# A fused linear, sigmoid and linear layer on one core: W2 staged through y, new places for Pool's loads, b2 added a stage sooner

## The reference

```python
# x: (1024, 24, 1024), W1: (1024, 24), b1: (1024,), W2: (1024, 1024), b2: (1024,), all float32
h = jax.nn.sigmoid(jnp.einsum('bts,st->bs', x, W1) + b1)
return h @ W2.T + b2
```

## Time and profile before

| | us |
|---|---|
| median of 3 runs | 336.53 |
| lowest, highest | 336.32, 337.71 |
| the profiled execution | 337.88 |
| its span, first to last instruction | 336.1 |

### The profile page before, as it was taken

The page is one execution under the profiler, slowest core; times in us unless marked ns, Lnnn a source line. Parts: engine busy times, 40 slices in busy tenths (PEclk is TensorE's granted clock), DMA queues, the critical chain, the costliest instruction groups (busy, mean ns, idle before and its releaser), DMA issues.

```text
span 336.1 us, 4849 instructions
## 1 busy us (share of the span) xinstructions
PE 273.2 (81%) x1825; PEld 238.0 (71%) x1825; DVE 259.1 (77%) x386; ACT 44.5 (13%) x76; POOL 165.5 (49%) x63
## 2 busy tenths in 40 slices
PE   2672975696977989999993899998889979299896
PEld 2572965596966877889782788876778868188674
DVE  0652997987998979799993489899788997168836
ACT  1210220211260000012300000040101140000010
POOL 0050007679059684800899980049755059972000
PEclk9978797977999999999997699999999998789979
DMA  8999959999999999999957999999999992698006
GB/s 260 398 398 393 387 183 393 386 387 387 386 386 387 387 387 387 387 384 373 373 205 244 374 375 384 383 385 374 373 373 372 356 341 81 207 345 262 1 0 250
DMA packets 67383, 109.99 MB, mean 327 GB/s; under 512 B 3224, under 2 KB 40096, under 8 KB 67360
## 3 DMA queue, kind: packets, MB, share of 16 engines
q1 hardware_dynamic: 65584, 106.96, 89.3%
q10 hardware_dynamic: 1776, 2.72, 2.2%
HBM read 105.48 MB, written 4.19 MB: 326 GB/s over the span
## 4 chain that ended last, share of the span: by engine, by line
PE 36%; DMA 35%; POOL 14%; issue 10%; ACT 2%; SPq 1%; DVE 1%; POOLq 0%; DVEq 0%; ACTq 0%
DMA ring<-in_r_x 35%; PE xbank L207 17%; PE pbank L267 15%; POOL y L463 6%; POOL nsum L446 3%; PE xbank L301 3%; POOL h_lo L456 2%; POOL nsum L451 1%; POOL nat L448 1%; PE pbank L301 1%; ACT h L392 1%; SPq L171 1%; DVE acc L323 1%; ACT h_hi L421 0%; PE pbank L225 0%
## 5 line engine op out<-in xcount | busy, mean ns | idle before, releaser
L323 DVE SCALAR_TENSOR_TENSOR acc<-xbank,w,acc 128x512 f32<-128x512 f32 x304 | 213.6, 746 | 57.1 <-PE xbank L207 54.5
L207 PE MATMUL xbank<-ident,ring 128*128 128x128 f32 x1280 | 190.8, 286 | 54.5 <-DMA ring<-in_r_x 53.6
L207 PEld LDWEIGHTS xbank<-ident,ring 128*128 128x128 f32 x1280 | 162.2, 149 | 83.2 <-issue 33.0
L448 POOL TENSOR_TENSOR nat<-nat,w1all 128x2048 f32<-128x2048 f32 (+2 forms) x15 | 55.1, 3674 | 50.7 <-DMA nat<-in_r_x 50.7
L451 POOL TENSOR_TENSOR nsum<-nsum,nat 128x2048 f32<-128x2048 f32 (+2 forms) x15 | 55.4, 3692 | 1.2
L267 PE MATMUL pbank<-w_hi,h_hi 128*128 128x512 f32 x112 | 51.7, 462 | 0.0
L267 PE MATMUL pbank<-w_lo,h_hi 128*128 128x512 f32 x112 | 50.8, 454 | 0.0
L456 POOL TENSOR_TENSOR h_lo<-h,h_hi 128x512 fp32r<-128x512 f32 x14 | 17.5, 1283 | 67.5 <-ACT h_hi L421 67.5
L267 PE MATMUL pbank<-w_hi,h_lo 128*128 128x512 f32 x112 | 45.6, 454 | 0.0
L446 POOL TENSOR_TENSOR nsum<-nat,w1all 128x2048 f32<-128x2048 f32 (+2 forms) x5 | 18.5, 3699 | 18.7 <-DMA nat<-in_r_x 18.7
L392 ACT ACTIVATE h<-acc,b1col 128x512 f32<-128x512 f32 (+1 forms) x19 | 11.0, 646 | 104.1 <-DVE y L339 57.7
(11 more groups left out here) (38 smaller groups left out, 94.7 us busy)
## 6 DMA issues: line engine op xcount, KB each, us to landing
ring<-in_r_x SPq DMA_DIRECT2D x40, 1024.0 KB, 14.4
ring<-in_r_x SPq DMA_DIRECT2D x40, 768.0 KB, 11.6
ring<-in_r_x SPq DMA_DIRECT2D x20, 512.0 KB, 7.5
nat<-in_r_x SPq DMA_DIRECT2D x8, 1024.0 KB, 14.2
nat<-in_r_x SPq DMA_DIRECT2D x8, 768.0 KB, 10.0
y<-in_L_rec_W SPq DMA_DIRECT2D x1, 2048.0 KB, 18.3
out_y<-y ACTq DMA_DIRECT2D x4, 512.0 KB, 6.8
nat<-in_r_x SPq DMA_DIRECT2D x4, 512.0 KB, 6.6
```

Of the source, the lines that this page charges most:

```text
L207: mm = pe.transpose(xbank[u % XBANKS][:, j * P:(j + 1) * P], tile[:, j, :], ident[:, :])
L323: nc.vector.scalar_tensor_tensor(out=acc[:, c, :], in0=xbank[u % XBANKS][:, :], scalar=w1[:, bass.ds((STAGES[i][1] + c) * T + t, 1)], in1= ...
L448: nc.gpsimd.tensor_tensor(slot, slot, row, ALU.mult).then_inc(nat_weighed, 1)
```

## The change

- STAGES gets the number of row tiles of a stage and a word for the fate of its outputs ("keep" in y, "add" to y, "last": add and store). Rows and chunks of the five stages stay as they were, and so do the fates.
- The places of Pool's four loads become (2, 4, 10, 14) in stage 0 and (0, 3, 10, 14) in the others. They were (3, 11, 15, 19) and (1, 6, 11, 16).
- W1 is the first load on SP's queue; it was the first on ACT's.
- W2's first half is loaded into y after place 1 and its second half into y after place 17 of stage 0, once SP has seen the eighth transpose of the first. Nothing of W2 goes through h and nat any more, and the wait of load m = 1 is gone. The transposes of W2 stand at units 14, 17, ..., 35 and 58, 61, ..., 79 (they stood at 12, 15, ..., 57); the second set of w1all rows stands between the two halves, at units 38 to 44 (it stood at 65 to 71).
- steps_due: the window begins at the same unit (10), but has 4/5 len - 10 units in place of len - 13: 57, 40, 40 and 23 units for 71, 50, 50 and 29.
- add_b2 stands ahead of low_parts in stages 1 and 3, and waits for the two kept outputs of a row tile and not for all eight.
- In the tail both chunks of the last h are made in pieces of 128 rows; it was the first chunk alone.

```diff
 STAGES = (
-    (0, 0, 4, (3, 11, 15, 19)),
-    (0, 4, 4, (1, 6, 11, 16)),
-    (1, 0, 3, (1, 6, 11, 16)),
-    (1, 3, 3, (1, 6, 11, 16)),
-    (1, 6, 2, (1, 6, 11, 16)),
+    (0, 4, 0, 4, (2, 4, 10, 14), "keep"),
+    (0, 4, 4, 4, (0, 3, 10, 14), "last"),
+    (4, 4, 0, 3, (0, 3, 10, 14), "keep"),
+    (4, 4, 3, 3, (0, 3, 10, 14), "add"),
+    (4, 4, 6, 2, (0, 3, 10, 14), "last"),
 )
...
         def steps_due(i, v):
 
-            lead, rest = 10, 3
-            span = len(units[i]) - lead - rest
-            return max(0, min(product_steps(i), -(-(v - lead + 1) * product_steps(i) // span)))
+            steps = outs[i - 1] * 3 * chunks[i - 1]
+            lead = 10 * JT // tiles[i]
+            span = (len(units[i]) * 4) // 5 - lead
+            return max(0, min(steps, -(-(v - lead + 1) * steps // span)))
...
-        W2_FROM, W2_EVERY = 12, 3
         SETS = {4 + q: q for q in range(1 + NK)}
-        SETS.update({65 + 2 * q: 1 + NK + q for q in range(NK)})
+        SETS.update({38 + 2 * q: 1 + NK + q for q in range(NK)})
+        W2S = {14 + 3 * m if m < SC else 58 + 3 * (m - SC): m for m in range(OH * SC)}
 
         @block.sync
         def _(sp):
+            sp.dma_start(w1[:, :].rearrange("p (c t) -> p c t", t=T),
+                         W1.rearrange("(c p) t -> p c t", p=P)).then_inc(w1_loaded, 16)
...
                     if at in places:
-                        if m == 1:
-                            sp.wait_ge(w2_turned, SC)
                         if m >= NATS:
                             sp.wait_ge(nat_freed, m - NATS + 1)
...
                     if i == 0 and at == 1:
-                        sp.dma_start(h[:, :, :].rearrange("p (j a) b -> p j (a b)", j=2), w2_v[1][:, 0:2, :]).then_inc(w2_loaded[1], 16)
-                        sp.dma_start(nat[:, 1, :, :].rearrange("p (j a) b -> p j (a b)", j=2), w2_v[1][:, 2:4, :]).then_inc(w2_loaded[2], 16)
-                    if i == 0 and at == 4:
                         sp.dma_start(y[:, :, :], w2_v[0]).then_inc(w2_loaded[0], 16)
+                    if i == 0 and at == 17:
+                        sp.wait_ge(w2_turned, SC)
+                        sp.dma_start(y[:, :, :], w2_v[1]).then_inc(w2_loaded[1], 16)
...
-            def add_b2(g):
+            def add_b2(b):
                 pool.wait_ge(b2_loaded, 16)
-                pool.wait_ge(part_kept, (g + 1) * OUTS)
                 for j in range(JT):
+                    pool.wait_ge(part_kept, kept_at[b] + OH * (j + 1))
                     nc.gpsimd.tensor_tensor(y[:, j, :], y[:, j, :], b2all[:, :], ALU.add).then_inc(b2_added, 1)
 
             for i in range(NS):
                 weighted_sum(i)
+                if i > 0 and fate[i - 1] == "keep":
+                    add_b2(i - 1)
                 if i < LAST:
                     low_parts(i)
-                if i in (1, 3):
-                    add_b2(i // 2)
```

More of the change, by code:

```diff
@@ L39, in rec_kernel @@
     XBANKS = 6
-    assert (B, T, S, O) == (2 * BANK, 24, 1024, 1024) and OUTS == 8
-    chunks = [s[2] for s in STAGES]
+    assert (B, T, S, O) == (2 * BANK, 24, 1024, 1024)
+    tiles = [s[1] for s in STAGES]
+    chunks = [s[3] for s in STAGES]
+    wide = [n * P for n in tiles]
+    fate = [s[5] for s in STAGES]
     units = []
-    ts = list(range(NK, T))
-    for g, c0, n, places in STAGES:
-        order = [("x", t, c) for t in ts[:-2] for c in range(n)]
+    for n in chunks:
+        order = [("x", t, c) for t in range(NK, T - 2) for c in range(n)]
         order += [("n", 0, c) for c in range(n)]
-        order += [("x", t, c) for t in ts[-2:] for c in range(n)]
+        order += [("x", t, c) for t in range(T - 2, T) for c in range(n)]
         units.append(order)
@@ L54, in rec_kernel @@
     first_h = [sum(chunks[:i]) for i in range(NS)]
+    outs = [OH * n for n in tiles]
+    first_out = [sum(outs[:i]) for i in range(NS)]
+    kept_at = [sum(n for n, f in zip(outs[:i], fate) if f == "keep") for i in range(NS)]
+    added_at = [sum(n for n, f in zip(outs[:i], fate) if f != "keep") for i in range(NS)]
     item_of, item_end = {}, []
     for i in range(NS):
-        for t in ts:
+        for t in range(NK, T):
             item_of[i, t] = len(item_end)
@@ L64, in chunk_end @@
         return first_unit[i] + max(v for v, (_, _, cc) in enumerate(units[i]) if cc == c) + 1
-    x_v = x.rearrange("(g j p) t s -> g p j t s", p=P, j=JT)
-    out_v = out.rearrange("(g j p) o -> g p j o", p=P, j=JT)
+    x_v = x.rearrange("(j p) t s -> p j t s", p=P)
+    out_v = out.rearrange("(j p) o -> p j o", p=P)
     w2_v = W2.rearrange("(h j p) s -> h p j s", p=P, j=JT)
@@ L97, in rec_kernel @@
         nat_loaded = [sem(f"nat_loaded{n}") for n in range(NATS)]
-        w2_loaded = [sem(f"w2_loaded{n}") for n in range(3)]
+        w2_loaded = [sem(f"w2_loaded{n}") for n in range(OH)]
         w1_loaded = sem("w1_loaded")
@@ L205, in turn_unit @@
                     tile = nsum[:, :, c * P:(c + 1) * P]
-                for j in range(JT):
+                for j in range(tiles[i]):
                     mm = pe.transpose(xbank[u % XBANKS][:, j * P:(j + 1) * P], tile[:, j, :], ident[:, :])
@@ L210, in turn_set @@
             def turn_set(q):
-                if q >= 2:
+                half, k = divmod(q - 1, NK)
+                if q == 1 + NK:
+                    pe.wait_ge(w_lo_ready, SC)
+                elif q >= 2:
                     pe.wait_ge(set_kept, q - 1)
@@ L310, in add_unit @@
                 kind, t, c = units[i][v]
-                n = chunks[i]
+                n, rows = chunks[i], slice(0, wide[i])
+                weight = w1[:, bass.ds((STAGES[i][2] + c) * T + t, 1)]
                 dve.wait_ge(unit_turned, u + 1)
@@ L411, in _ @@
                     act.wait_ge(unit_added, chunk_end(i, c))
-                    if i == LAST and c == 0:
-                        for j in range(JT):
+                    if i < LAST:
+                        sigmoid(i, c, slice(0, wide[i]))
+                    else:
+                        for j in range(tiles[i]):
                             sigmoid(i, c, slice(j * P, (j + 1) * P))
-                    else:
-                        sigmoid(i, c)
                 if i < LAST:
-                    act.wait_ge(out_summed, OUTS * i)
+                    act.wait_ge(out_summed, first_out[i])
                     for c in range(chunks[i]):
                         act.wait_ge(h_ready, first_h[i] + c + 1)
-                        nc.scalar.copy(h_hi[:, c, :], h[:, c, :]).then_inc(h_hi_ready, 1)
+                        nc.scalar.copy(h_hi[:, c, :wide[i]], h[:, c, :wide[i]]).then_inc(h_hi_ready, 1)
         @block.gpsimd
```

190 lines of the change are left out of this document (84 added, 106 removed).

## The result

The changed kernel takes **322.07 us** (median of 4 runs, 321.23 to 322.97) where the kernel before takes 337.12: a ratio of 0.9555, 95% interval 0.9512 to 0.9598, or 15.1 us less. The forecast was 315.4, with a stated range of 309.5 to 323. The profiled execution took 322.97 us with a span of 321.2.

The account below looks back on a forecast made before the run. The kernel was taken as a DMA load stream with three holes, PE and DVE close beside it. Stage terms -3.5, -1.0, -7.9, +0.5, -9.2 and tail 0 sum to -21.1, from 336.53 to 315.4 us; range 309.5 to 323.

Parts of the forecast that it names:

- b2 and the holes: Stages 2 and 4: b2 added a stage sooner lets Pool multiply earlier; stage totals, dense window included, -7.9 and -9.2 us.
- the likeliest one: Whole kernel: the forecast's own case, 315.4 us with own range 311 to 319.5; chance 0.62.
- All three signs that I had named for "wrong": PE waiting for ring mid-stages 2 to 4, granted clock falling in the windows, or first boundary after 93.7 us.
- the term of 1 us: Stage 4's start: ninth item lands late, near +12 against +11.4 us wanted; 1 us booked, bounds 0 and 4.
- 4.5 us in my sum: Stage 4: multiply ends at boundary +7.5 us, the ninth item lands near +12.
- the rival "Pool's wait comes back at place 10": SP's third nat load still waits for Pool; PE stands 3 us in stages 2, 3 and 4: 324.5 us; chance 0.18.
- the ring's lead: Stage 2: ring holds six items, so a dry queue of 0 to 2 us does not reach PE.
- 3.5 us at the first boundary: Stage 0: new load order without SP emptying the queue brings the boundary to 90.2 instead of 93.7 us.
- The dense window: Stages 1 to 4: fewer window units cost time where PE and DVE bound; stage 2 53.6 us, against 51.7 modelled before.
- W1 first: Stage 0: DVE starts near 8 us but waits for the third item at 20.1, so worth 0.
- The bound of 9.7 us: Stage 0: W1's full landing time delays x, ending stage 0 9.1 us later; rival at 324.5 us, chance 0.04.
- The tail: a term that I put at nothing: Tail: same matmuls, 16.6 us as before, change 0; nothing booked against the longer rest of each stage.

Follow-up runs that it names:

- the kernel with other places in stage 4: Changed kernel with Pool's four loads of stage 4 at places 0, 3, 12, 16 instead of 0, 3, 10, 14: 320.83 us, ratio 0.9521.
- longer window: Changed kernel with product steps spread over len - 13 units again instead of 4/5 len - 10: 320.09 us, ratio 0.9501.
- W2 early: Changed kernel with W2 loaded early through h, nsum and y without SP's wait, stage 0 nat places 5, 9, 15, 18: 326.92 us, ratio 0.9681.
- b2 late: Changed kernel with Pool adding b2 behind the low parts at the boundary again: 340.25 us, ratio 1.009.
- new places alone: Kernel before with only places 0, 3, 10, 14 in stages 1 to 4: 341.27 us, ratio 1.0123.
- W1 on ACT: Changed kernel with W1 first on ACT's queue again instead of SP's: 321.50 us, ratio 0.9558.
- stage 0 as before: Changed kernel with the whole of stage 0's earlier order put back, W1 staying first on SP: 328.92 us, ratio 0.9755.
- stores cut on the changed kernel: Changed kernel storing 128 instead of 1,024 columns of the first 512 output rows in stage 2, the rest unwritten: 322.84 us.
- the old places in the changed kernel: Changed kernel with places 1, 6, 11, 16 again in stages 1 to 4: 320.56 us, ratio 0.9513.

## Why the prediction was right, and where it was not

**b2 and the holes: right in mechanism.** The multiply begins 6.4 and 5.1 us after the boundary, SP's waits are 7 us, stage 2 took 54.4 us where 53.6 were forecast, and putting b2 back costs 18 us. The kind of case is the likeliest one, but the time lies outside the range of 311 to 319.5 that this case had for itself. It lies in the stated range, and luck had a part in that: the stages missed by + 10.1 us (0, 2, 3 and 4) and - 3.9 us (1 and the tail), and the tail's part is a clock that the changed kernel seldom gets (below). All three signs that I had named for "wrong" came: PE waited for ring in stage 4 (3.35 us), the clock fell in its window (0.50 from 278 to 280 us), and the first boundary came at 94.0.

**The slow restart in stage 4: the term of 1 us was mis-sized.** It is 4.8 us by the kernel with other places in stage 4 (43.8 against 39.0), and above its bound of 4. I let the ninth item land at boundary + 12 us. It landed at 277.9, + 15.6. The multiply came when I had it (269.85, + 7.5). What failed is the time from SP's issue to landing, 4.5 us in my sum and 8.05 in the trace:

```profile
269.88 0.37 SPq L169 DMA_DIRECT2D nat<-in_r_x  x1
270.29 4.03 SPq L175 DMA_DIRECT2D ring<-in_r_x  x3
```

```profile
268.00:270.00 2.00, 2.00 (x13) 1.00 0.26 92
270.00:272.00 2.00, 2.00 (x15) 1.00 0.46 115
272.00:274.00 2.00, 2.00 (x15) 1.00 1.01 356
274.00:276.00 2.00, 0.57 (x3) 1.00 1.09 368
276.00:278.00 2.00, 0.07 (x1) 0.90 1.04 341
278.00:280.00 2.00, 2.00 (x7) 0.50 1.06 346
```

The queue is dry from 268 us (92 and 115 GB/s in two stretches of 2 us), and then moves some 0.35 MB a microsecond. By the landing of the ninth item at 277.8 it has moved 2.3 MB, where the nat load and the ninth item are 1.05 MB. So by then much of what SP issued behind them has come in as well. By the trace's times from issue to landing the nat load alone took 6.5 us (it landed at 276.4), and the ninth and tenth items followed 1.4 us behind each other (277.8 and 279.2). Why the first one took so long isn't shown. In the seven other kernels that stand at place 10 in stage 4 the nat load took 3.6 to 4.2 us, and the pair 5.25, 5.5, 5.8, 5.9, 6.5, 6.8 and 7.0 us (longer window, W2 early, b2 late, new places alone, W1 on ACT, stage 0 as before, stores cut on the changed kernel). So the 8.05 is the high end, and a term of 4.5 would have been too small in each. The wait of 3.35 us also brought the half clock (0.50 from 278 to 280 us); with W1 on ACT the wait was 1.25 us, the clock stayed, and stage 4 took 41.0 us. The places moved by two items take the wait away whole (39.0 us); with the longer window 0.79 us of it stayed (40.4 us). This was the rival "Pool's wait comes back at place 10", for one stage and not for three; in stage 2 the ring's lead covered a dip to 312 GB/s as counted.
The Trainium skill, page "DMA: Bandwidth & Descriptors", section "Anatomy of one DMA — SWDGE (gpsimd) path", gives a load some 2 us fixed and its bytes at 436 GB/s, on the path that it describes; by these figures I estimate 2.0 + 2.4 = 4.4 us for the pair, near the 4.5 of my sum. It is another path than SP's, and the measured 5.25 to 8.05 us decide.

**Stage 0: the wrong place and the wrong reason.** I booked 3.5 us at the first boundary. It did not move (94.0 for 93.7). 2.2 us of the miss are that the item behind W2's second half landed at 68.5 and not 66.3 us: I had taken 2.64 us a megabyte from the first 32 us, where the page shows 393 to 407 GB/s, and the stream goes on at 387, 2.71 us; and the third item was 0.7 us late. DVE started 1.1 us behind the item and not 0.7, and its 28 units and 8 parts of w_lo took 24.4 us where I had 23.2 (0.92 us of it is one more wait for PE at 73 us). But the 4.4 us of stream that the hole had cost were saved all the same, and came out in stage 1 (62.6 for 65.9 us, where I had 64.9). In stage 1 PE waited 6.0 us for ring before the change, 3.5 us with stage 0 as before, and not once in the changed kernel, where it is busy 62.53 of 62.55 us. So the stream set that stage before, and PE and DVE set it now, as my sum had it, with 2.3 us too much. The two stages together: forecast -4.5, measured 159.6 - 156.6 = -3.0 us; undoing them, +4.7 us at the second boundary. The step that failed is the accounting: I looked for the stream's gain at the end of the stage that was edited, and it showed where PE had waited for loads, a stage later.

**The dense window: a cost where I had one, but not in the place.** My model had it at 53.6 - 51.7 = 1.9 us in stage 2 and about 1 in stage 4. The ratios (0.9555 and 0.9501, intervals that overlap) give 1.8 us in all. It isn't in stage 2, which starts late on loads in both versions (5.1 us and more to the first product step) and is 54.4 and 55.5 us. In the profiled executions it is in stage 4, by the landing of the ninth item, and for that no run ties the cause to the window. One place where the window does act is the tail, next.

**W1 first: right.** The medians with and without it differ by 0.6 us, less than their intervals can tell, and the first boundary by 0.6 us (94.0 and 93.4). The bound of 9.7 us is refuted.

**The tail: a term that I put at nothing, and luck in this execution.** I forecast 16.6 us as before, since the matmuls are the same, and booked nothing against the longer rest. It took 15.1 us, at a clock of 1.00. For the same 48 matmuls the fourteen profiled executions fall into three groups: 15.0 to 15.1 us five times (clock 0.96 or 1.00 over the tail), 16.5 to 16.7 six times (0.90, the kernel before among them), 17.7 to 17.8 three times (0.79). Where it is 17.7, the clock is 0.50 from the tail's first matmul on; three of the six of 16.5 to 16.7 us start so too, by the time of their first matmul (0.76 us and not 0.47), and are back at full speed sooner. PE stands ahead of the tail, and how long depends on the window: 3.64 or 3.65 us in the eight kernels with the dense window, 2.34 to 2.44 us in the six with the longer one (the kernel before and the one with the new places alone are among these). Here is the tail's first matmul with the old places in the changed kernel, and in the kernel before:

```profile
301.94 0.77 PE L291 MATMUL pbank<-w_hi,h_hi 128*128 128x512 f32 x1 [3.65 <-DVE h_lo L348]
```

```profile
320.01 0.50 PE L301 MATMUL pbank<-w_hi,h_hi 128*128 128x512 f32 x1 [2.34 <-DVE h_lo L358]
```

With the dense window the tail took 15.1 us once, 16.5 to 16.7 four times and 17.7 to 17.8 three times, a mean of 16.8; with the longer one 15.0 to 15.1 four times and 16.6 twice, a mean of 15.6. That makes some 1.2 us of cost for the dense window, a term that my sum didn't have, from one profiled execution of each kernel. The mean clocks of whole executions go the same way: 0.950 to 0.963 in the four of the changed kernel, 0.968 to 0.978 in the four with the longer window. What decides the clock within each group was not tried.

**Shares.** By medians and ratios: b2's move 18.2 us, stage 0's order 6.8, the new places 4 lost in the kernel before and 1.5 in the changed one, the dense window 1.8 lost; the last two are not clear of noise. As each is taken with all others in place, they don't have to add up to 15.1.

## What to carry to other kernels

An in-order queue that waits for a slow engine is a hole in the stream even where that engine is idle half of the time: look at what stands between the event and the instruction that frees the buffer, and move the work that nobody waits for (here b2) out of that stretch. Look at how many loads stand ahead of the one that waits: one place sooner cost 4 us in the kernel before, and two places later took PE's wait in stage 4 away. And when loads set the pace, book a gain on the stream and carry it on until something stops it; the boundary nearest to the edit may not move at all.

## What the runs showed of the hardware

- From the issue of a 512 KB nat load on a queue that had nearly run dry to the landing of the 512 KB item behind it, it took 5.25 to 8.05 us (eight executions), where 1.05 MB at 350 GB/s are 3.0 us.
- The stream's rate was 386 GB/s with row pieces of 2 KB (stages 0 and 1), 373 with 1.5 KB and 348 with 1 KB. The size of a load fell with the piece (1 MB, 768 KB, 512 KB), so which of the two it is isn't shown.
- PE's granted clock fell to 0.50 behind a wait of 3.35 us in stage 4. The tail ran at 1.00, 0.90 or 0.79 behind a wait of 3.65 us, and at 1.00, 0.96 or 0.90 behind one of 2.3 to 2.4 us: steps of 1.1 to 1.6 us, as large as some effects of this study.
